# Attention's dense layer in fp16 parts, interleaved with the last attention groups, on one Trainium2 core

## What is computed

```python
x = x + 0.5 * ffn(layernorm(x), w1, mean_w1, w2, mean_w2, w3, mean_w3)
x = x + attn(layernorm(x), w_qkv, b_qkv, w_dense, b_dense)
x = x + 0.5 * ffn(layernorm(x), ...)          # the same weights
# ffn: W = mean + mean(|w - mean|) * sign(w - mean);  (silu(h W1) * (h W3)) W2, 1792 wide
# attn: 32 query heads of 16 on 8 KV heads, rope, causal softmax(q k^T / 16) v, then
#       out = ctx @ w_dense.T + b_dense
```

## Time and profile before

| | us |
|---|---|
| median of 3 runs | 1590.66 |
| the profiled execution | 1592.39 |
| its span | 1590.7 |
| TensorE busy | 1474.8 |
| VectorE busy | 873.8 |
| ScalarE busy | 643.4 |
| GpSimd busy | 149.9 |

### The profile page before, as it was taken

How to read it: one execution, slowest core, us unless ns; L and a number is a source line. 1 busy time by engine, 2 the same in 40 slices (tenths; PEclk the granted TensorE clock), 3 DMA queues, 4 the chain that set the end, 5 groups by cost and what they waited for, 6 DMA issues and landing times.

```text
span 1590.7 us, 25041 instructions
## 1 busy us (share of the span) xinstructions
PE 1474.8 (93%) x9584; PEld 659.8 (41%) x9584; DVE 873.8 (55%) x1375; ACT 643.4 (40%) x903; POOL 149.9 (9%) x217
## 2 busy tenths in 40 slices
PE   0788999899999987799999999989999999999998
PEld 0233444344444443334343444324444444444443
DVE  7979432432544476899999999923431422412212
ACT  4464111121122254388888888781211112112111
POOL 0320000000000143012121212210000000000000
PEclk9989999999999998599999999999999999999999
DMA  9501800000000001000000000024000000000000
GB/s 389 195 0 53 354 0 0 1 0 0 1 0 1 1 1 34 1 2 2 2 2 3 2 3 2 2 102 177 0 0 0 28 0 0 27 0 1 27 0 27
DMA packets 16459, 57.38 MB, mean 36 GB/s; under 512 B 4848, under 2 KB 4848, under 8 KB 15856
## 3 DMA queue, kind: packets, MB, share of 16 engines
q1 hardware_dynamic: 16368, 56.11, 9.1%
HBM read 40.63 MB, written 15.20 MB: 35 GB/s over the span
## 4 chain that ended last, share of the span: by engine, by line
PE 83%; DVE 9%; ACT 3%; issue 3%; DMA 0%; POOL 0%; DVEq 0%; ACTq 0%; POOLq 0%
PE ps L1232 32%; PE ps L1253 16%; PE ps L1491 9%; PE ps L1406 7%; PE ps L1472 5%; PE ps L1393 3%; PE ps L1589 3%; PE ps L1279 2%; PE ps L1226 1%; DVE rowmax L1120 1%; PE ps L1501 1%; DVE wbase L877 1%; ACT probs L706 1%; PE ps L1365 1%; DVE w_raw L842 1%
## 5 line engine op out<-in xcount | busy, mean ns | idle before, releaser
L1232 PE MATMUL ps<-xt_hi,w_all 128*128 128x512 f16 x896 | 283.3, 388 | 42.3 <-DVE w_all L883 19.7
L706 ACT ACTIVATE probs<-ps 128x1024 f32<-128x1024 f32 (+3 forms) x384 | 294.1, 814 | 48.5 <-PE ps L1472 45.5
L1120 DVE TENSOR_REDUCE rowmax<-ps 128x2 f32<-128x1024 f32 (+3 forms) x208 | 237.1, 1140 | 15.7 <-PE ps L1414 7.4
L971 DVE SCALAR_TENSOR_TENSOR hb<-ps,scal,silub 128x512 f32<-128x512 f32 x56 | 42.0, 751 | 266.6 <-PE ps L1232 266.6
L1406 PE MATMUL ps<-ka,qa 48*128 48x512 f16 (+3 forms) x768 | 165.7, 345 | 15.4 <-DVE rowmax L1120 9.2
L1232 PE MATMUL ps<-xt_lo,w_all 128*128 128x512 f16 x448 | 173.9, 388 | 0.0
L1491 PE MATMUL ps<-probs,vs 128*32 128x512 f32 (+3 forms) x1536 | 164.4, 500 | 1.4 <-ACT ctx_sb L725 0.8
L1232 PEld LDWEIGHTS ps<-xt_hi,w_all 128*128 128x128 f16 (+1 forms) x896 | 89.4, 100 | 155.9 <-issue 46.0
L1124 DVE TENSOR_REDUCE rowmax<-ps 128x1 f32<-128x512 f32 x192 | 131.2, 684 | 16.3 <-PE ps L1406 13.5
L1472 PE MATMUL ps<-qa,ka 50*128 50x512 f16 (+3 forms) x768 | 133.3, 330 | 3.7 <-ACT probs L706 3.0
L1253 PE MATMUL ps<-w32b_all,hhib 128*128 (+1 forms) x448 | 133.3, 379 | 0.0
(11 more groups left out here) (154 smaller groups left out, 2160.8 us busy)
## 6 DMA issues: line engine op xcount, KB each, us to landing
spill<-w_all SPq DMA_DIRECT2D x1, 10752.0 KB, 28.8
w32b_all<-spill SPq DMA_DIRECT2D x1, 7168.0 KB, 20.9
x<-x_in SPq DMA_DIRECT2D x4, 1024.0 KB, 5.3
y_out<-x SPq DMA_DIRECT2D x4, 1024.0 KB, 4.2
wbase<-m1t SPq DMA_DIRECT2D x4, 896.0 KB, 12.7
w_raw<-w1t SPq DMA_DIRECT2D x4, 896.0 KB, 14.2
wbase<-m3t SPq DMA_DIRECT2D x4, 896.0 KB, 24.3
w_raw<-w3t SPq DMA_DIRECT2D x4, 896.0 KB, 24.3
```

The lines of the kernel that those rows point to most:

```text
L706: nc.scalar.activation(probs[u % PBUF][:, 2 * pair:2 * pair + 2, 0:q1 - q0], wide(("scores", g, (u, pair)))[:, :, 0:q1 - q0], ACT.Exp, sca ...
L971: nc.vector.scalar_tensor_tensor(out=bufs["h"][u][:, :], in0=ps[:, UP, :], scalar=scal[:, 1:2], in1=bufs["silu"][u][:, :], op0=ALU.mult, o ...
L1120: nc.vector.tensor_reduce(dst, src, AX.X, ALU.max).then_inc(pair_taken, 1)
L1232: last = mm(ps[:, bank, :], w[a][:, k, bass.ts(t, P)], xt[b][:, k, :], start=(k == 0 and n == 0), stop=(k == HB - 1 and n == 2))
```

## The change

- Dense's weight (wd_raw, fp32) is turned into a scaled high and low fp16 part. In group 0 ScalarE sums magnitudes (a bound), GpSimd reduces it over the partitions, VectorE makes a power-of-two scale (dense_scale), ScalarE scales the weight in place and copies the high parts (dense_high); GpSimd subtracts for the low parts in group 1 (dense_low). They are written to four free places (wd_at) and SP copies them to wd_raw's place after group 7's rows.
- The column of ones beside v holds a scale instead of 1, so context comes out scaled; scal[:, 4:5] undoes both scales when dense is added to x.
- bias_x moves to GpSimd, two tiles in each of the iterations k = 2 to 9.
- The loop over k ends after k = 15 on TensorE and VectorE. What was k = 16 and 17 is written out, with dense of batch 0's tiles 0 to 7 between its scores and values, in quarters (project(i, q) is three fp16 products). transpose_rows(i) and project(i) now use the same bank, rows_bank(i). High and low parts of a context tile are made by VectorE for tiles 0 to 7; for tiles 8 to 15 ScalarE makes the high part.
- Layer norm 8's statistics are taken one tile at a time in this stretch, its transposes come at tiles 10 and 11. Every layer norm's Newton step is three operations instead of four.
- FFN 2 waits for x2_ready before its first down instead of before its first gate.

```diff
@@ -219,13 +219,16 @@
-    mrow = at("mrow", [8 * SEQ_TILES, P], F16, C0 + 6144)
+    mrow = at("mrow", [8 * SEQ_TILES, P], F16, B0 + 34816)
...
-    wd = at("wd", [P, HB, HID], F32, R0)
+    wd_raw = at("wd_raw", [P, HB, HID], F32, R0)
+    wd_at = [at(f"wd_at{i}", [P, 2, HID], F16, a) for i, a in enumerate((D0 + 6144, D0 + 14336, B0 + 30720, C0 + 6144))]
+    wd = [at(f"wd_{n}", [P, HB, HID], F16, R0 + 4096 * i) for i, n in enumerate(("hi", "lo"))]
     bd = at("bd", [P, HID], F32, R0 + 8192)
-    ctx_t = [at(f"ctx_t{i}", [P, HB, P], F32, R0 + 10240 + i * 2048) for i in range(2)]
+    ctx_t = [[at(f"ctx_t{n}{i}", [P, HB, P], F16, R0 + 10240 + i * 2048 + j * 1024) for j, n in enumerate(("hi", "lo"))]
+             for i in range(2)]
     assert R0 + 14336 == D0
...
@@ -328,6 +333,10 @@
         return WIDE[use] + 1
+    def rows_bank(i):
+        return PAIR_BANK + i % 2
...
@@ -374,7 +383,7 @@
         sp.wait_ge(v_ready, TOKEN_TILES)
-        sp.dma_start(wd[:, :, :], wdt.rearrange("(t p) n -> p t n", p=P)).then_inc(wd_loaded, 16)
+        sp.dma_start(wd_raw[:, :, :], wdt.rearrange("(t p) n -> p t n", p=P)).then_inc(wd_loaded, 16)
...
@@ -385,6 +394,11 @@
                     .then_inc(m_placed, 16)
+            if g == 7:
+                sp.wait_ge(wdlo_ready, HB)
+                for i in range(2):
+                    for n in range(2):
+                        sp.dma_start(wd[i][:, 2 * n:2 * n + 2, :], wd_at[2 * i + n][:, :, :]).then_inc(wd_placed, 16)
...
@@ -466,7 +480,9 @@
                 nc.gpsimd.memset(vs[i][:, :, HEAD + 1:32], 0.0).then_inc(ones_ready, 1)
-                nc.gpsimd.memset(vs[i][:, :, HEAD:HEAD + 1], 1.0).then_inc(ones_ready, 1)
+                chain(nc.gpsimd.memset(vs[i][:, :, HEAD:HEAD + 1], 1.0))
+                nc.gpsimd.tensor_scalar(vs[i][:, :, HEAD:HEAD + 1], vs[i][:, :, HEAD:HEAD + 1], wc[:, 4, 4:5], None,
+                                        ALU.mult).then_inc(ones_ready, 1)
...
@@ -492,9 +508,32 @@
 
+        def dense_low(n):
+            pool.wait_ge(wdhi_ready, n // 2 + 1)
+            nc.gpsimd.tensor_tensor(out=wd_at[2 + n // 2][:, n % 2, :], in0=wd_raw[:, n, :], in1=wd_at[n // 2][:, n % 2, :],
+                                    op=ALU.subtract).then_inc(wdlo_ready, 1)
+        def dense_bound():
+            pool.wait_ge(part_ready, 5)
+            nc.gpsimd.partition_all_reduce(allr[:, 3, 1:2], part[:, 3, 1:2], P, RMAX).then_inc(allr_ready, 1)
+        def bias_x(i):
+            nc.gpsimd.tensor_tensor(out=x[:, i, :], in0=x[:, i, :], in1=bd[:, :], op=ALU.add).then_inc(bias_ready, 1)
         for k in range(GROUPS + 2):
             mask_unit(k - 2, 7)
             mask_unit(k - 2, 8)
+            if k == 0:
+                dense_bound()
+            if k == 1:
+                for n in range(HB):
+                    dense_low(n)
+            if 2 <= k < 10:
+                bias_x(2 * (k - 2))
+                bias_x(2 * (k - 2) + 1)
...
@@ -724,12 +763,32 @@
 
+        def dense_magnitude():
+            act.wait_ge(wd_loaded, 32)
+            nc.scalar.activation(probs[0][:, :, :].rearrange("p h q -> p (h q)"),
+                                 wd_raw[:, :, :].rearrange("p t n -> p (t n)"), ACT.Abs,
+                                 accum_out=part[:, 3, 1:2]).then_inc(part_ready, 1)
+        def dense_high():
+            act.wait_ge(wd_scaled, 1)
+            act.wait_ge(part_ready, 5)
+            nc.scalar.activation(wd_raw[:, :, :].rearrange("p t n -> p (t n)"),
+                                 wd_raw[:, :, :].rearrange("p t n -> p (t n)"), ACT.Copy, scale=wc[:, 3, 3:4])\
+                .then_inc(wd_unit, 1)
+            act.wait_ge(wd_unit, 1)
+            for n in range(2):
+                nc.scalar.copy(wd_at[n][:, :, :], wd_raw[:, 2 * n:2 * n + 2, :]).then_inc(wdhi_ready, 1)
             take_qk(k + 1, 0)
+            if k == 0:
+                dense_magnitude()
...
@@ -756,20 +815,21 @@
+            if k == 0:
+                dense_high()
...
+        def context_high(i):
             act.wait_ge(dt_full, i + 1)
+            act.wait_ge(dense_full, i - 1)
+            nc.scalar.copy(ctx_t[i % 2][0][:, :, :].rearrange("p a b -> p (a b)"), ps[:, rows_bank(i), :])\
+                .then_inc(ctx_hi_ready, 1)
+        for i in range(SEQ_TILES, TOKEN_TILES):
+            context_high(i)
+            if i in (10, 11):
+                ln_hi(8, 2 * (i - 10))
+                ln_hi(8, 2 * (i - 10) + 1)
         ffn(1, ffn2)
...
@@ -784,29 +844,40 @@
-                chain(nc.vector.tensor_tensor(out=b, in0=a, in1=var, op=ALU.mult))
-                chain(nc.vector.tensor_scalar(a, b, -0.5, 1.5, ALU.mult, ALU.add))
-                chain(nc.vector.tensor_tensor(out=y, in0=y, in1=a, op=ALU.mult))
-            chain(nc.vector.tensor_scalar(rstd[:, m, :], y, XS, None, ALU.mult))
+                chain(nc.vector.scalar_tensor_tensor(out=b, in0=a, scalar=-0.5, in1=var, op0=ALU.mult, op1=ALU.mult))
+                chain(nc.vector.scalar_tensor_tensor(out=y, in0=b, scalar=1.5, in1=y, op0=ALU.add, op1=ALU.mult))
+            chain(nc.vector.tensor_scalar(rstd[:, n % 4, :], y, XS, None, ALU.mult))
...
@@ -1161,7 +1232,14 @@
+        def dense_scale():
+            dve.wait_ge(allr_ready, 9)
+            chain(nc.vector.tensor_copy(wc[:, 3, 1:2], allr[:, 3, 1:2]))
+            power_of_two(3)
+            nc.vector.tensor_tensor(out=scal[:, 4:5], in0=wc[:, 3, 4:5], in1=wc[:, 4, 4:5], op=ALU.mult).then_inc(wd_scaled, 1)
...
+        for k in range(GROUPS):
...
@@ -1180,6 +1258,8 @@
+            if k == 0:
+                dense_scale()
...
@@ -1192,23 +1272,72 @@
+        def context_high(i):
+            dve.wait_ge(dt_full, i + 1)
+            if i >= 2:
+                dve.wait_ge(dense_full, i - 1)
+            nc.vector.tensor_copy(ctx_t[i % 2][0][:, :, :].rearrange("p a b -> p (a b)"), ps[:, rows_bank(i), :])\
+                .then_inc(ctx_hi_ready, 1)
+        def context_low(i):
+            dve.wait_ge(ctx_hi_ready, i + 1)
+            hi, lo = (t[:, :, :].rearrange("p a b -> p (a b)") for t in ctx_t[i % 2])
+            nc.vector.tensor_tensor(out=lo, in0=ps[:, rows_bank(i), :], in1=hi, op=ALU.subtract).then_inc(ctx_lo_ready, 1)
+        def add_dense(i):
             dve.wait_ge(dense_full, i + 1)
             dve.wait_ge(bias_ready, i + 1)
+            nc.vector.scalar_tensor_tensor(out=x[:, i, :], in0=ps[:, rows_bank(i), :], scalar=scal[:, 4:5], in1=x[:, i, :],
+                                           op0=ALU.mult, op1=ALU.add).then_inc(x2_ready, 1)
+        context_high(0)
+        context_low(0)
+        context_high(1)
+        context_low(1)
+        dve.wait_ge(wd_scaled, 1)
+        add_dense(0)
+        dve.wait_ge(x2_ready, 1)
+        norm_rows(8, 0)
+        context_high(2)
+        context_low(2)
+        add_dense(1)
+        normalise(14, 0)
...
+        context_high(5)
+        context_low(5)
+        normalise(15, 0)
+        dve.wait_ge(x2_ready, 4)
+        norm_rows(8, 3)
+        add_dense(4)
+        norm_seed(8)
+        norm_newton(8)
+        context_high(6)
+        context_low(6)
+        add_dense(5)
+        normalised(8)
+        context_high(7)
+        context_low(7)
+        add_dense(6)
+        normalise(15, 1)
+        context_low(SEQ_TILES)
+        add_dense(7)
+        for i in range(SEQ_TILES, TOKEN_TILES):
+            if i + 1 < TOKEN_TILES:
+                context_low(i + 1)
+            add_dense(i)
+            if i in (10, 11):
+                ln_lo(8, 2 * (i - 10))
+                ln_lo(8, 2 * (i - 10) + 1)
...
@@ -1299,6 +1428,8 @@
                             pe.wait_ge(resid_ready, TPC * (CHUNKS * f + c))
+                        elif f:
+                            pe.wait_ge(x2_ready, TOKEN_TILES)
                         down(T0 + t - 1, t - 1, (t - 1) % 2, wc_, bufs, t == 1, False)
...
@@ -1504,7 +1635,7 @@
             transpose_qk(0, o)
-        for k in range(GROUPS + 2):
...
@@ -1575,34 +1706,139 @@
         def transpose_rows(i):
             b, tt = divmod(i, SEQ_TILES)
-            if i >= 2:
-                pe.wait_ge(ctx_t_ready, i - 1)
...
+            if tt % 4 == 0:
+                pe.wait_ge(single_taken, taken(("ctx", GROUPS * (b + 1) // BATCH - 1, tt // 4)))
+            if i == 0:
+                pe.wait_ge(pair_taken, NPAIR * GROUPS)
+            elif i >= 2:
                 pe.wait_ge(x2_ready, i - 1)
             for q in range(HB):
-                last = mm(ps[:, i % 2, :], ctx_t[i % 2][:, q, :], wd[:, q, :], start=(q == 0), stop=(q == HB - 1))
...
+                last = tr(ps[:, rows_bank(i), q * P:(q + 1) * P], context[:, tt, q, b, :], ident[:, :])
+            last.then_inc(dt_full, 1)
+        def project(i, q):
+            if i == 0 and q == 0:
+                pe.wait_ge(wd_placed, 64)
+            if q == 0:
+                pe.wait_ge(ctx_hi_ready, i + 1)
+                pe.wait_ge(ctx_lo_ready, i + 1)
+            for n, (a, b) in enumerate(PASSES):
```

(151 more changed lines are left out.)

52 lines of the change are left out of this document (17 added, 35 removed).

## The result

The changed kernel took 1570.63 us (median of 4 runs, 1569.09 to 1571.40), the kernel before 1590.99 (1590.39 to 1592.07) on the same chip: a ratio of 0.987, 95% interval 0.9853 to 0.9887, 20.4 us less. The forecast was 1565.5, the range 1561.5 to 1574: right in direction and inside the range, 5 us too low.

A forecast was written before the change was run, and what follows sets the result against it. The prediction took FFN 2's first gate, behind TensorE's holes in late attention and dense alone, to set the time: -25.8 + 1.5 + 0.3 - 1.2 = -25.2 us from the 1590.66 us median, 1565.5 us; range 1561.5 to 1574.

The forecast's parts named there:

- Stretch A: Unit (14, 7)'s first score to project(7, 3)'s end: 48.1 us of TensorE work plus 0.5 of waits, ending at 1088.1.
- the price list: TensorE's start-to-start prices: values 1.00 us, score pair 0.22, fp16 product 0.216, four fp32 transposes 0.44.
- rival 1: The in-order tail, dense among attention, waits more than walked: 11 us more, 1576.5 us, or 1571 for half; chance 0.17.
- Stretch B: Dense's tiles 8 to 15: 25.6 us of TensorE work plus waits, 28.8 us in all, ending at 1116.9.
- the bank wait: Dense's tiles 8 to 15: tile i+2 is transposed into the bank tile i's sum is read from; 0.33 us for six tiles, 2.0.
- The holes: Attention's last groups: 9 us of TensorE holes in 32 us; interleaved, ScalarE stops being the bound and the clock stays 2.4 GHz.
- dense_scale: Group 0: eight chained small VectorE operations before piece 17 cost 1.5 us; magnitude, high and low parts 0.3 more.
- Newton's step: Layer norm: three operations fewer, 0.6 us, in the open at the start and for norm 7 in QKV; 1.2 us less.
- Bias additions: Groups 2 to 9: two GpSimd additions need 3 us in an idle gap of 8.67; cost taken as 0, at worst 12 us.
- Rival 2: GpSimd's work reaches the path in groups 1 to 9: 2 to 12 us more, 1567.5 to 1577.5; chance 0.10.
- The weight load: FFN 2's w3/w2 load: 20.9 us from normalise(15, 1) at 1086.7, landing at 1107.7, hidden, 9 us ahead of 1116.9.
- Up to QKV: Start of the kernel to QKV's first product: 0.6 us less forecast.

The follow-up runs named there:

- switch_probe: Changed kernel plus extra TensorE products ahead of FFN 2: 128-row products and 50-row pairs alternating, then the same products sorted by shape; 1586.39 us.
- half: Changed kernel with the quarters of dense's product for tiles 0 to 7 put together to two halves; 1569.00 us.
- whole: Changed kernel with dense's tiles 0 to 6 in one piece each, own PSUM banks for tiles 8 to 15 and layer norm 8's transposes later; 1569.48 us.
- banks: Changed kernel with the sums of dense's tiles 8 to 15 in two PSUM banks of their own; 1568.37 us.
- dense_after: Changed kernel without the interleaving: attention's last groups in the old order, then all sixteen dense tiles in fp16 parts; 1581.44 us.
- newton3_alone: Kernel before with nothing but the three-operation Newton step; 1588.70 us against 1591.50, ratio 0.9982.
- bias_nm: Changed kernel with one GpSimd bias addition behind unit 6's mask in each of groups 2 to 15, two staying in the old place; 1602.61 us.

## Why the prediction was right, and where it wasn't

- *Stretch A*, 53.6 us where 48.6 stood. The failed term is the price list: each price was taken between operations of one kind. The trace has 31 score pairs with dense or a transpose behind them (0.10 us more each), 22 pieces of products with scores or values behind them (0.10), and ten groups of transposes before these (0.59 us for 0.44 to 0.5): 3.1 + 2.2 + 1.2 = 6.5 us. The sum had 0.7 for issues and 0.5 for waits, of which 0.16 came: by this estimate 5.5 more, 5.0 measured. switch_probe shows the first of the three prices by itself, and half and whole show that A gets shorter with fewer pieces. The hint stood in the earlier trace rows, 0.57 us from a transpose to a score, and was named in rival 1 but left out of the sum. Rival 1 gave the right size (1571 for half of it) and the right rows, with a wrong mechanism for the most part: nothing waits longer than 0.16 us.
- *Stretch B* 28.8 us, as forecast. banks shows that 1.94 of it are the bank wait (forecast 2.0). A tile takes 3.44 us (1095.08 to 1098.52), not 3.3.
- *The holes*: ScalarE no longer bounds A, and the clock stays at 1.00. dense_after shows the place to be worth 10.3 us.
- *dense_scale*: 0.9 us in group 0, the same in all twelve traces that have it; 1.5 + 0.3 were forecast, and part of the eight operations fell in idle time (0.38 us before the next piece in the kernel before, at 645.00).
- *Newton's step*: the chain's 0.6 us in QKV are there. Of the 0.6 at the start only the start is there (wc's first operation at 34.63, before 35.28): at QKV's first product newton3_alone is at 533.35, the kernel before at 533.15. That the clock gives 1.4 more in QKV was missed, though the earlier trace rows showed the low clock behind a stand.
- *Bias additions*: nothing, as forecast, at this place. Rival 2's price was too low: 12 us as the worst case, for additions in 8 groups, where bias_nm with 14 lost 32, since half of that is the clock behind the waits.
- *The weight load* was issued at 1089.24 and landed after 20.4 us, 9.8 ahead of the gate (forecast 9). *The gate* waits for nothing.
- *Up to QKV* 1.3 us more were gained than forecast in this pair. The start of QKV varies by 2.4 us between kernels with the same lists, so no gain up to there is shown, and why it varies stays open.

The total is 5 us above the forecast as A is; in the profiled pair the early stretches (-1.9 - 2.2 + 0.9 + 0.7 = -2.5 us against a forecast of +0.6) hid part of it, in the medians less. That is luck: nothing in the sum stood for it. QKV and group 0, which repeat in all traces, came out 2.5 us better than forecast; without them the time would be some 1573 us (an estimate), just inside the range.

## What to carry to other kernels

Before work of one shape is put between work of another on TensorE, price each change (0.10 us here) and make the pieces as long as the engine that feeds the old work can bear: halves of a tile gained 0.9 us over quarters, whole tiles lost 1.7 against halves. When work is moved to GpSimd, look at which small SBUF operation of VectorE it will lie over and who waits for that: such additions cost nothing in one gap and 32 us in all when they stand 3.3 us earlier in 14 groups. A shorter stand of TensorE can be worth more than its length, since the clock behind it can be better too: 0.6 us less were worth 2.0 in QKV.
